# Attention scores on the two row halves of the TensorE array: eight heads per unit in place of four

## The chip, the cores and the metric

The kernel runs on one core of a Trainium2 chip. The metric is the device time of one execution in microseconds (us); lower is better. Engines are named as in the profile: PE is TensorE (PEld its weight loads), DVE is VectorE, ACT is ScalarE, POOL is GpSimd, SP issues DMAs.

## The reference

Thirty-two batches of 128 tokens of width 512 go through a layernorm, a cross-attention with 32 heads of width 16, a residual, a second layernorm and a mixture of eight experts with two chosen per token. The part that matters here is the attention of one batch: own keys and values, and a second set (the adapter's) from `ctx`, with its own softmax and a gate per head.

```python
scores = einsum('bhqd,bhkd->bhqk', q, k) * inv_sqrt_d + attention_mask
w = softmax(scores)
attn_output = einsum('bhqk,bhkd->bhqd', w, v)
a_scores = einsum('bhqd,bhkd->bhqk', q, a_k) * inv_sqrt_d
a_scores = tanh(gate) * softmax(a_scores)
attn_output = attn_output + einsum('bhqk,bhkd->bhqd', a_scores, a_v)
return attn_output.transpose(0, 2, 1, 3).reshape(bsz, q_len, hid) @ Wo
```

## The kernel before

Two phases: attention with the router, one batch of 128 tokens per step, then the experts, 71 slots of 128 tokens. The change touches the first. Its order is written out by hand: each engine has a function `step(b, c, d, n, m)` that is called for each batch b, and in it works on b, on the batch before (d), the one before that (c), the next (n) and the one after (m). Engines meet at semaphores (`wait_ge`, `then_inc`); an engine that waits holds everything behind it in its own order.

**Heads as pairs.** Queries and keys are split into two float16 parts, so a head takes 64 rows: two heads, a pair, fill the 128 partitions. `stack` (PE, L1084) transposes two pairs of queries, keys and adapter keys at a time (group g, four heads) into bank ma0 or ma1; `stack_out` (ACT, L553 and L555) copies them to qz and kk. In qz an even head has its rows 0 to 63 and zeros below, an odd head rows 64 to 127 and zeros above, so both use the same full-height key block.

**Maxima for n.** `adapter_scores` (L1108) and `own_scores` (L1117) make the scores of group g with queries on the partitions in md1 and md0; `maxima` (DVE, L754, L756, L759) adds the mask and takes the maximum over keys. PE's scores of group g wait for DVE's maxima of group g-1, since the banks are the same. `neg_max` splits minus the maxima into three bfloat16 parts, `max_turn` turns them, and mT holds them with heads on the rows.

**Transposed scores for b.** Units u = 0 to 15: g = u // 2 is the group of four heads, path = u % 2 is own or adapter. `scores_T` (L1143 to L1152) fills bank st[path]: two matmuls of 256 columns for the scores, on path 0 two of 512 for the mask (`mskp`, in two parts), and four of 128 that subtract the maximum through the selector `hsel`. `exps` (ACT, L561) takes the exponential of the bank to pr; `values` (L1166) multiplies by the values, four heads in four column strips of the array. A unit's bank is filled again two units later, after the exponential of u-2.

PE's step goes through u = 0 to 15: scores of u, then what lies at that place of batches n and d, then `values(u-1)`:

```python
for u in range(2 * GROUPS):
    scores_T(b, u)
    ...
    if n and u in STACK_AT:
        stack(n, STACK_AT.index(u))
    if n and u in SCORES_AT:
        adapter_scores(n, SCORES_AT.index(u))
    if u:
        values(b, u - 1)
    ...
```

Ahead of u = 0 is the query projection of n (`q`), at u = 2 the key projection `k`, at u = 3 the output projection of d, at u = 4 the adapter's keys `ak`, at u = 7 `h_turn`, at u = 8 `router`, and after u = 15 the values' projection `v`, `adapter_scores(7)`, `values(15)`, `own_scores(7)`, the adapter's values `avp` and `max_turn`. `v` waits for `stack_out` of group 6, the last user of ma0. `normal` (DVE) divides by the sums, eight heads at a time (o), after `values_back`. Lines are those of the kernel before.

Of the kernel before, what the change touches and what calls it, by code (L numbers as in the profile page):

```python
# [45 lines left out]
STACK_AT = (6, 7, 8, 9, 10, 11, 13, 15)  # L46
SCORES_AT = (8, 9, 10, 11, 12, 13, 14)
# [56 lines left out]
def attention_phase(nc, ctx, dram, keep):  # L104
# [25 lines left out]
    hsel = sb("hsel", [3 * NH, NH], BF16)  # L130
# [24 lines left out]
    mx = sb("mx", [P, 2, NH], F32)  # L155
    mr = sb("mr", [P, 2, NH], F32)
    mp = sb("mp", [P, 2, 3, NH], BF16)
    mT = sb("mT", [3 * NH, 2, P], BF16)
# [205 lines left out]
    def _(pool):  # L364
# [124 lines left out]
    def _(act):  # L489
# [56 lines left out]
        def stack_out(n, g):  # L546

            act.wait_ge(t_pe.sem, t_pe.at(n.shift(-1), 2 * g + 2))
            act.wait_ge(stk_t.sem, stk_t.at(n, g + 1))
            bank, pairs = half(ma[g % 2]), slice(2 * g, 2 * g + 2)  # L550
            for j in range(2):
                r = slice(64 * j, 64 * j + 64)
                act.activation(qz[r, pairs, j, :], bank[r, 0:2], ACT.Copy)  # L553
            keys = bank[:, 2:6].rearrange("p (k a) n -> p k a n", k=2)
            act.activation(kk[:, :, pairs, :], keys, ACT.Copy).then_inc(stk_o.sem, 1)  # L555

        def exps(n, u):
            path = u % 2
            act.wait_ge(t_pe.sem, t_pe.at(n, u + 1))
            act.wait_ge(av_pe.sem, av_pe.at(n, u - 1))  # L560
            act.activation(pr[:, path, :, :], st[path][:, :, :], ACT.Exp).then_inc(p_ex.sem, 1)  # L561
# [103 lines left out]
    def _(dve):  # L665
# [30 lines left out]
        pool_c_all = 19  # L696
# [53 lines left out]

        def maxima(n, g):
            dve.wait_ge(s_pa.sem, s_pa.at(n, g + 1))
            dve.wait_ge(s_own.sem, s_own.at(n, g))
            dve.tensor_reduce(mx[:, 1, 4 * g:4 * g + 4], sm[1][:, :, :], AX.X, ALU.max).then_inc(s_ad.sem, 1)  # L754
# [4 lines left out]
            dve.tensor_reduce(mx[:, 0, 4 * g:4 * g + 4], sm[0][:, :, :], AX.X, ALU.max).then_inc(s_own.sem, 1)  # L759

        def neg_max(n, b=None):
# [4 lines left out]
            p3 = [mp[:, :, k, :] for k in range(3)]  # L766
# [13 lines left out]
            dve.tensor_copy(mT[:, :, :], m_bank()[0:3 * NH]).then_inc(m_T.sem, 1)  # L780

        def normal(n, o):

            bank = av[o % 2][:, :, :].rearrange("p (a g) (j c) -> p a (g j) c", a=2, c=VC)
# [3 lines left out]
            dve.tensor_tensor(rc[:, 1, :], rc[:, 1, :], tg[:, 8 * o:8 * o + 8], ALU.mult).then_inc(n_rg.sem, 1)  # L788
# [4 lines left out]
            if o == 0:  # L793
                if whole(n):
# [3 lines left out]
            dve.tensor_tensor(heads(on)[:, 8 * o:8 * o + 8, :], part2[:, 0, :, :], part2[:, 1, :, :],  # L798
                              ALU.add).then_inc(n_o.sem, 1)
# [235 lines left out]
    def _(pe):  # L1035
# [88 lines left out]
        def max_turn(n):  # L1124
            pe.wait_ge(mp3.sem, mp3.at(n))
            for path in range(2):
                i = pe.transpose(m_bank()[0:3 * NH, path, :], mp[:, path, :, :].rearrange("p a h -> p (a h)"),
                                 ident_bf[:, :])
            i.then_inc(mp_t.sem, 1)

        def scores_T(n, u):

            g, path = u // 2, u % 2
            if u == 0:
# [15 lines left out]
            for j in range(4):  # L1150
                h = 4 * g + j
                i = pe.matmul(bank[:, j, :], hsel[:, h:h + 1].to_broadcast([3 * NH, P]), mT[:, path, :],  # L1152
                              start=False, stop=(j == 3), skip_group_check=True)
            i.then_inc(t_pe.sem, 1)

        def values(n, u):
            g, path = u // 2, u % 2
# [4 lines left out]
            if u % 4 == 0:  # L1162
                pe.wait_ge(n_o.sem, n_o.at(n, u // 4 - 1))
            for j in range(4):
                h = 4 * g + j
                i = pe.matmul(av[u // 4 % 2][VC * j:VC * j + VW, 2 * path + g % 2, :], vv[:, n.par, path, h, :],  # L1166
                              pr[:, path, j, :], start=True, stop=True)
# [464 lines left out]
```

## Time and profile before

| | us |
|---|---|
| median of 3 runs | 2137.03 |
| lowest, highest | 2134.46, 2138.43 |
| the profiled execution's own time | 2133.7 |
| its span, first to last instruction | 2131.9 |

Busy over the span: PE 89%, PEld 55%, DVE 68%, ACT 57%, POOL 30%. The attention phase ends some 1645 us into the span. A busy share counts a matmul from its start to its modelled end; matmuls overlap, so the starts tell more than the share.

### The profile page before, as it was taken

How to read it: one execution, taken by the hardware profiler on the slowest of the kernel's cores; microseconds unless marked ns; L12 is line 12 of the kernel's file. 1: busy time of each engine (PE TensorE's matmuls, PEld its weight loads, DVE VectorE, ACT ScalarE, POOL GpSimd, SP SyncE). 2: the span in 40 equal slices, each digit the busy share in tenths (PEclk: the TensorE clock that was granted, in tenths of full speed). 3: DMA queues.
4: the chain of work that ended last, by engine and by line, in shares of the span. 5: the costliest groups of instructions: out<-in, count | busy, mean ns of one | idle time of the engine just before them, and what ended most of it. 6: DMA issues, size and time to landing. Idle time of an engine off the chain costs nothing. (4 is left out here: it accounts for less than half of the span.)

```text
span 2131.9 us, 54083 instructions
## 1 busy us (share of the span) xinstructions
PE 1900.5 (89%) x18697; PEld 1172.2 (55%) x18698; DVE 1452.3 (68%) x3621; ACT 1219.3 (57%) x2228; POOL 647.5 (30%) x667
## 2 busy tenths in 40 slices
PE   4898899989998999999899999999983799999997
PEld 2555555555554555555555555555551466666664
DVE  5577788888887888888788888888874333333332
ACT  4565566666665666666566666666662434434342
POOL 3123233222322222232222222222321344444443
PEclk8999999999999999999999999999996899999999
DMA  3011111111111111111111111111012444444443
GB/s 124 24 34 34 34 34 34 40 41 55 35 34 35 34 34 34 34 34 39 30 40 52 45 34 34 34 34 34 29 33 72 106 81 86 82 83 85 81 87 59
DMA packets 64040, 106.14 MB, mean 50 GB/s; under 512 B 19089, under 2 KB 23185, under 8 KB 63313
## 3 DMA queue, kind: packets, MB, share of 16 engines
q0 software_dynamic: 18144, 37.31, 9.7%
q1 hardware_dynamic: 45680, 65.96, 9.6%
q8 instruction: 136, 2.23, 0.4%
q14 instruction: 80, 0.65, 0.1%
HBM read 67.51 MB, written 35.72 MB: 48 GB/s over the span
## 5 line engine op out<-in xcount | busy, mean ns | idle before, releaser
L561 ACT ACTIVATE pr<-st 128x512 f32<-128x512 f32 x512 | 299.9, 592 | 202.9 <-PE st L1152 193.0
L1499 PE MATMUL y<-w1s,hgT 128*128 x1704 | 279.8, 314 | 3.7 <-ACT hgT L1413 3.7
L410 POOL TENSOR_TENSOR t<-t 128x512 f32<-128x512 f32 x32 | 50.4, 1575 | 668.6 <-DVE t L734 668.6
L754 DVE TENSOR_REDUCE mx<-md 128x4 f32<-128x512 f32 x256 | 176.6, 690 | 86.6 <-PE md L1108 71.9
L1166 PE MATMUL av<-pr,vv 128*17 128x128 f32 x4096 | 212.4, 278 | 17.5 <-ACT pr L561 17.1
L1499 PEld LDWEIGHTS y<-w1s,hgT 128*128 128x128 f16 x1704 | 164.4, 98 | 95.4 <-issue 4.1
L553 ACT ACTIVATE qz<-ma 64x256 f16<-64x256 f16 x512 | 191.7, 374 | 19.2 <-PE ma L1084 16.2
L1152 PE MATMUL st<-mT,hsel 96*128 96x128 bf16 x2048 | 201.8, 221 | 0.0
L1143 PE MATMUL st<-qz,kk 128*128 128x256 f16 x1024 | 197.8, 275 | 1.4 <-DVE mT L780 1.4
L759 DVE TENSOR_REDUCE mx<-md 128x4 f32<-128x512 f32 x256 | 177.0, 691 | 8.7
L1147 PE MATMUL st<-identr,mskp 128*128 128x512 f32 x512 | 182.3, 437 | 0.0
L1152 PEld LDWEIGHTS st<-mT,hsel 96*128 96x128 bf16 x2048 | 137.5, 98 | 75.7 <-issue 69.8
L756 DVE TENSOR_TENSOR md<-md,msk 128x512 f32<-128x512 f32 x256 | 177.1, 692 | 0.0
L1413 ACT ACTIVATE hgT<-px 128x1024 f16<-128x1024 f16 x71 | 72.7, 1024 | 155.7 <-PE px L1489 155.7
L555 ACT ACTIVATE kk<-ma 128x512 f16<-128x512 f16 x256 | 152.9, 597 | 3.0
L1518 PE MATMUL y<-w2s,yT 128*128 (+1 forms) x639 | 150.3, 379 | 0.9 <-DVE yT L1477 0.9
L1117 PE MATMUL md<-kk,qz 128*128 128x128 f16 x1024 | 101.1, 221 | 51.3 <-DVE mx L759 50.9
L1476 DVE COPY yT<-py 128x256 f16<-128x256 f16 x142 | 40.4, 284 | 148.2 <-PE py L1508 148.2
L405 POOL TENSOR_TENSOR xcs<-nat,xcs 128x512 f16<-128x512 f32 x31 | 36.0, 1162 | 300.3 <-ACT xcs L493 300.3
L1166 PEld LDWEIGHTS av<-pr,vv 128*17 128x17 f32 x4096 | 68.2, 95 | 103.2 <-issue 54.1
L1117 PEld LDWEIGHTS md<-kk,qz 128*128 128x128 f16 x1024 | 60.3, 97 | 110.1 <-issue 110.1
L1392 POOL DMA_INDIRECT out<-yo,dst x71 | 113.2, 1594 | 16.9 <-issue 12.6
(210 smaller groups left out, 3999.6 us busy)
## 6 DMA issues: line engine op xcount, KB each, us to landing
wst<-in_w SPq DMA_DIRECT2D x32, 352.0 KB, 3.2
cin<-in_ctx SPq DMA_DIRECT2D x32, 256.0 KB, 3.8
xin<-in_x SPq DMA_DIRECT2D x32, 256.0 KB, 3.4
xres<-in_x SPq DMA_DIRECT2D x32, 256.0 KB, 3.6
out<-x SPq DMA_DIRECT2D x32, 256.0 KB, 2.1
h_pairs<-ohs SPq DMA_DIRECT2D x32, 256.0 KB, 2.1
msk<-in_mask SPq DMA_DIRECT2D x32, 64.0 KB, 3.4
lrow<-lists SPq DMA_DIRECT2D x71, 1.0 KB, 3.5
```

Source lines behind the costliest of these rows:

```text
L553: act.activation(qz[r, pairs, j, :], bank[r, 0:2], ACT.Copy)
L555: act.activation(kk[:, :, pairs, :], keys, ACT.Copy).then_inc(stk_o.sem, 1)
L561: act.activation(pr[:, path, :, :], st[path][:, :, :], ACT.Exp).then_inc(p_ex.sem, 1)
L754: dve.tensor_reduce(mx[:, 1, 4 * g:4 * g + 4], sm[1][:, :, :], AX.X, ALU.max).then_inc(s_ad.sem, 1)
L756: dve.tensor_tensor(sm[0][:, :, :], sm[0][:, :, :], msk[:, n.par, :].unsqueeze(1).to_broadcast([P, 4, P]), ALU.add).then_inc(s_mask.sem, 1)
L759: dve.tensor_reduce(mx[:, 0, 4 * g:4 * g + 4], sm[0][:, :, :], AX.X, ALU.max).then_inc(s_own.sem, 1)
L1117: i = pe.matmul(sm[0][:, j, :], qz[:, h // 2, h % 2, :], kst[:, h // 2, :], start=True, stop=True)
L1143: pe.matmul(bank[:, 2 * j:2 * j + 2, :], keys[:, p, :], qz[:, p, :, :], start=(j == 0), stop=False, skip_group_check=True)
L1147: pe.matmul(bank[:, :, :], mskp[:, n.par, part, :], identr[:, :].unsqueeze(1).to_broadcast([P, 4, P]), start=False, stop=False, skip_group ...
L1152: i = pe.matmul(bank[:, j, :], hsel[:, h:h + 1].to_broadcast([3 * NH, P]), mT[:, path, :], start=False, stop=(j == 3), skip_group_check=True)
L1166: i = pe.matmul(av[u // 4 % 2][VC * j:VC * j + VW, 2 * path + g % 2, :], vv[:, n.par, path, h, :], pr[:, path, j, :], start=True, stop=True)
L1499: i = pe.matmul(y1[s.par][j][:, 0:F], hgT[:, s.par, a, c, :], w, start=(n == 0), stop=(n == 11))
```

## The change

A unit of scores now has eight heads of one path. Even heads of four pairs go to bank st0 with array rows 0 to 63, odd heads to st1 with rows 64 to 127; each matmul has 64 rows and 128 columns, and the two halves alternate. The maxima are laid out likewise: even heads on rows 0 to 63 of mT, odd ones on 64 to 127, and `hsel` selects within a half. There are eight calls `scores_T(n, w)`, at the even places u = 2w; each raises `t_pe` twice. `exps` and `values` stay at sixteen, now with path = u // 2 % 2 and r = u % 2, the bank. `scores_T(w)` waits for both exponentials of w-1. The masks' matmuls of path 0 stand ahead of the scores. `stack_out(g)` waits for the scores of all eight heads that use its block, and stack 6 moves from u = 13 to u = 14, scores of group 6 from u = 14 to u = 15.

```diff
-STACK_AT = (6, 7, 8, 9, 10, 11, 13, 15)
-SCORES_AT = (8, 9, 10, 11, 12, 13, 14)
+STACK_AT = (6, 7, 8, 9, 10, 11, 14, 15)
+SCORES_AT = (8, 9, 10, 11, 12, 13, 15)
...
-        for part in range(3):
+        for k in range(6):
             const(pool.affine_select(out=hsel[:, :], in_=hsel[:, :], compare_op=ALU.not_equal, fill=1.0,
-                                     base=-NH * part, pattern=[[-1, NH]], channel_multiplier=1))
+                                     base=-(64 * (k // 3) + PAIRS * (k % 3)), pattern=[[-1, PAIRS]],
+                                     channel_multiplier=1))
+        const(pool.memset(mp[:, :, :], 0.0))
...
-            act.wait_ge(t_pe.sem, t_pe.at(n.shift(-1), 2 * g + 2))
+            act.wait_ge(t_pe.sem, t_pe.at(n.shift(-1), 4 * (g // 2) + 4))
...
-        pool_c_all = 19
+        pool_c_all = 23
...
+        def largest(path, g):
+
+            into = mx[:, 2 * path:2 * path + 2, 2 * g:2 * g + 2].rearrange("q r p -> q p r")
+            of = sm[path][:, :, :].rearrange("q (p r) k -> q p r k", r=2)
+            return dve.tensor_reduce(into, of, AX.X, ALU.max)
...
-        def scores_T(n, u):
-
-            g, path = u // 2, u % 2
-            if u == 0:
+        def scores_T(n, w):
+
+            o, path = w // 2, w % 2
+            if w == 0:
                 pe.wait_ge(m_T.sem, m_T.at(n))
                 pe.wait_ge(m_lo.sem, m_lo.at(n))
                 pe.wait_ge(m_hi.sem, m_hi.at(n))
-            if u >= 2:
-                pe.wait_ge(p_ex.sem, p_ex.at(n, u - 1))
-            bank, keys = st[path], (kst, akst)[path]
-            for j in range(2):
-                p = 2 * g + j
-                pe.matmul(bank[:, 2 * j:2 * j + 2, :], keys[:, p, :], qz[:, p, :, :], start=(j == 0), stop=False,
-                          skip_group_check=True)
+            else:
+                pe.wait_ge(p_ex.sem, p_ex.at(n, 2 * w))
             if path == 0:
-                for part in range(2):
-                    pe.matmul(bank[:, :, :], mskp[:, n.par, part, :],
-                              identr[:, :].unsqueeze(1).to_broadcast([P, 4, P]), start=False, stop=False,
-                              skip_group_check=True)
+                for r in range(2):
+                    for part in range(2):
+                        pe.matmul(st[r][:, :, :], mskp[:, n.par, part, :],
+                                  identr[:, :].unsqueeze(1).to_broadcast([P, 4, P]), start=(part == 0), stop=False,
+                                  skip_group_check=True)
             for j in range(4):
-                h = 4 * g + j
-                i = pe.matmul(bank[:, j, :], hsel[:, h:h + 1].to_broadcast([3 * NH, P]), mT[:, path, :],
-                              start=False, stop=(j == 3), skip_group_check=True)
-            i.then_inc(t_pe.sem, 1)
+                for r in range(2):
+                    rows, p = slice(64 * r, 64 * r + 64), 4 * o + j
+                    pe.matmul(st[r][:, j, :], (kst, akst)[path][rows, p, :], qz[rows, p, r, :],
+                              start=(path == 1 and j == 0), stop=False, skip_group_check=True)
+            for j in range(4):
+                for r in range(2):
+                    rows, p = slice(64 * r, 64 * r + 64), 4 * o + j
+                    i = pe.matmul(st[r][:, j, :], hsel[rows, p:p + 1].to_broadcast([64, P]), mT[rows, path, :],
+                                  start=False, stop=(j == 3), skip_group_check=True)
+                    if j == 3:
+                        i.then_inc(t_pe.sem, 1)
...
             for u in range(2 * GROUPS):
-                scores_T(b, u)
+                if u % 2 == 0:
+                    scores_T(b, u // 2)
```

The rest of the diff gives `mx`, `mr`, `mp`, `mT` and `hsel` the new layout and has `normal`, `values` and `exps` read heads in it; their counts and sizes stay, but for mT, which is copied with 128 rows in place of 96.

PE around u = 7 and 8, before (st is a bank of scores, L1174 is `values_back`, L1084 a stack, L1108 adapter scores for the maxima; `h_turn` and `router` stand here only where there is a batch d):

```order
L1143 MATMUL st<-qz,kk 128x256 x2
L1152 MATMUL st<-mT,hsel 128x128 x4
L1174 MATMUL av<-identr,avT 128x128 x4
L1084 MATMUL ma<-ident,qs 128x128 x2
L1084 MATMUL ma<-ident,ks 128x128 x2
L1084 MATMUL ma<-ident,aks 128x128 x2
L1166 MATMUL av<-pr,vv 17x128 x4
L1143 MATMUL st<-qz,kk 128x256 x2
L1147 MATMUL st<-identr,mskp 128x512 x2
L1152 MATMUL st<-mT,hsel 128x128 x4
L1084 MATMUL ma<-ident,qs 128x128 x2
L1084 MATMUL ma<-ident,ks 128x128 x2
```

and after (L1160 and L1165 are the scores and the maxima of a unit, L1154 the mask, L1096 a stack, L1120 adapter scores):

```order
L1187 MATMUL av<-identr,avT 128x128 x4
L1096 MATMUL ma<-ident,qs 128x128 x2
L1096 MATMUL ma<-ident,ks 128x128 x2
L1096 MATMUL ma<-ident,aks 128x128 x2
L1179 MATMUL av<-pr,vv 17x128 x4
L1154 MATMUL st<-identr,mskp 128x512 x4
L1160 MATMUL st<-qz,kk 128x128 x8
L1165 MATMUL st<-mT,hsel 128x128 x8
L1096 MATMUL ma<-ident,qs 128x128 x2
L1096 MATMUL ma<-ident,ks 128x128 x2
L1096 MATMUL ma<-ident,aks 128x128 x2
L1120 MATMUL md<-kk,qz 128x128 x4
```

Between stack 0 and the adapter scores of group 0 there were two units, of four heads each, one with and one without the mask; now there is one, with four mask matmuls and sixteen of 128 columns.

PE from the last scores of u = 14 to the values' projection, before (L1117 is own scores, L1045 on w_v the projection):

```order
L1152 MATMUL st<-mT,hsel 128x128 x4
L1174 MATMUL av<-identr,avT 128x128 x4
L1108 MATMUL md<-kk,qz 128x128 x4
L1166 MATMUL av<-pr,vv 17x128 x4
L1117 MATMUL md<-kk,qz 128x128 x4
L1143 MATMUL st<-qz,kk 128x256 x2
L1152 MATMUL st<-mT,hsel 128x128 x4
L1084 MATMUL ma<-ident,qs 128x128 x2
L1084 MATMUL ma<-ident,ks 128x128 x2
L1084 MATMUL ma<-ident,aks 128x128 x2
L1166 MATMUL av<-pr,vv 17x128 x4
L1045 MATMUL ma<-w_v,xT 128x512 x12
```

and after, from `values_back` at the same place (the unit of scores ahead of it is L1160 x8 and L1165 x8):

```order
L1187 MATMUL av<-identr,avT 128x128 x4
L1096 MATMUL ma<-ident,qs 128x128 x2
L1096 MATMUL ma<-ident,ks 128x128 x2
L1096 MATMUL ma<-ident,aks 128x128 x2
L1179 MATMUL av<-pr,vv 17x128 x4
L1096 MATMUL ma<-ident,qs 128x128 x2
L1096 MATMUL ma<-ident,ks 128x128 x2
L1096 MATMUL ma<-ident,aks 128x128 x2
L1120 MATMUL md<-kk,qz 128x128 x4
L1179 MATMUL av<-pr,vv 17x128 x4
L1129 MATMUL md<-kk,qz 128x128 x4
L1057 MATMUL ma<-w_v,xT 128x512 x12
```

The unit of u = 15 is gone, and stack 6 now stands here, two rows ahead of stack 7; the adapter scores of group 6, which read its copy, come right behind stack 7 and ahead of the projection.

## Rows read from the trace of the kernel before

**Rows 1.** The page, part 1: busy time of each engine, share of the span, instructions.

```profile
PE 1900.5 (89%) x18697; PEld 1172.2 (55%) x18698; DVE 1452.3 (68%) x3621; ACT 1219.3 (57%) x2228; POOL 647.5 (30%) x667
```

**Rows 2.** Waits of PE over the span: who for whom, total us, times, longest.

```profile
PE md L1117 <- DVE mx L759: 50.9, 130, 0.9
PE ma L1084 <- DVE aks L721: 37.6, 32, 2.6
```

**Rows 3.** Windows: stretch, its us, busy us (instructions) by engine, clock, DMA.

```profile
1389.33:1437.62 48.29, 44.50 (x483) 27.39 (x482) 40.47 (x94) 31.67 (x61) 12.94 (x11) 1.00 0.11 38
1415.08:1431.84 16.76, 15.12 (x209) 10.74 (x207) 15.90 (x29) 12.81 (x29) 3.31 (x4) 1.00 0.07 21
```

**Rows 4.** Timeline of PE, one step, first part: start us, us, instruction, [idle before].

```profile
1389.33 2.75 PE L1045 MATMUL ma<-w_q,xT 128*128 128x512 f16 x12
1391.92 0.38 PE L1143 MATMUL st<-qz,kk 128*128 128x256 f16 x2
...
1392.85 0.38 PE L1143 MATMUL st<-qz,kk 128*128 128x256 f16 x2
...
1393.86 0.41 PE L1166 MATMUL av<-pr,vv 128*17 128x128 f32 x8 [0.40 <-ACT pr L561]
...
1395.14 2.75 PE L1045 MATMUL ma<-w_k,xT 128*128 128x512 f16 x12
...
1403.94 2.75 PE L1045 MATMUL ma<-w_k,cT 128*128 128x512 f16 x12
```

**Rows 5.** Timeline of ACT in the same step: exponentials, adapter keys.

```profile
1393.13 1.09 ACT L561 ACTIVATE pr<-st 128x512 f32<-128x512 f32 x2 [1.80 <-PE st L1152]
...
1406.73 1.02 ACT L519 ACTIVATE aks<-ma 128x1024 f16<-128x1024 f32 x1 [1.70 <-PE ma L1045]
```

**Rows 6.** Timeline of PE in the same step, middle part.

```profile
1410.05 0.27 PE L1084 MATMUL ma<-ident,qs 128*128 128x128 f16 x2 [1.08 <-DVE aks L721]
...
1410.47 0.41 PE L1166 MATMUL av<-pr,vv 128*17 128x128 f32 x8
1410.82 0.39 PE L1143 MATMUL st<-qz,kk 128*128 128x256 f16 x2
...
1411.27 0.61 PE L1174 MATMUL av<-identr,avT 128*128 128x128 f32 x4
...
1413.86 0.45 PE L1045 MATMUL md<-rw,hT 128*128 128x8 f16 x12
1414.17 0.27 PE L1084 MATMUL ma<-ident,qs 128*128 128x128 f16 x2
...
1414.66 0.38 PE L1108 MATMUL md<-kk,qz 128*128 128x128 f16 x4
```

**Rows 7.** Timeline of ACT in the same step: first stack copied out, exponential.

```profile
1410.58 0.77 ACT L553 ACTIVATE qz<-ma 64x256 f16<-64x256 f16 x2 [0.35 <-PE ma L1084]
1411.36 0.60 ACT L555 ACTIVATE kk<-ma 128x512 f16<-128x512 f16 x1
1411.85 0.59 ACT L561 ACTIVATE pr<-st 128x512 f32<-128x512 f32 x1
```

**Rows 8.** Timeline of DVE in the same step: adapter keys, maxima of groups 0, 4.

```profile
1408.51 1.28 DVE L721 SCALAR_TENSOR_TENSOR aks<-ma,aks 128x512 f16<-128x512 f32 x2
...
1415.08 0.69 DVE L754 TENSOR_REDUCE mx<-md 128x4 f32<-128x512 f32 x1 [0.57 <-PE md L1108]
...
1424.62 0.69 DVE L754 TENSOR_REDUCE mx<-md 128x4 f32<-128x512 f32 x1
```

**Rows 9.** Timeline of PE in the same step, last part.

```profile
1422.53 0.38 PE L1117 MATMUL md<-kk,qz 128*128 128x128 f16 x4 [0.60 <-DVE mx L759]
...
1426.78 0.38 PE L1117 MATMUL md<-kk,qz 128*128 128x128 f16 x4 [0.40 <-DVE mx L759]
...
1430.49 2.76 PE L1045 MATMUL ma<-w_v,xT 128*128 128x512 f16 x12
```

**Rows 10.** Timeline of POOL at the program's start.

```profile
6.57 0.92 POOL L385 TENSOR_SCALAR_AFFINE_SELECT hsel<-hsel 96x32 bf16<-96x32 bf16 x3
```

More of the change, by code:

```diff
@@ L129, in attention_phase @@
     ones = sb("ones", [P, P], BF16)
-    hsel = sb("hsel", [3 * NH, NH], BF16)
+    hsel = sb("hsel", [P, PAIRS], BF16)
     rope = sb("rope", [P, 4, HD], F32)
@@ L154, in attention_phase @@
     vv = sb("vv", [P, 2, 2, NH, VW], F32)
[L155 to L158, printed above, removed]
+    mx = sb("mx", [P, 4, PAIRS], F32)
+    mr = sb("mr", [P, 4, PAIRS], F32)
+    mp = sb("mp", [P, 2, P], BF16)
+    mT = sb("mT", [P, 2, P], BF16)
     pr = sb("pr", [P, 2, 4, P], F32)
@@ L557, in exps @@
         def exps(n, u):
-            path = u % 2
+            r = u % 2
             act.wait_ge(t_pe.sem, t_pe.at(n, u + 1))
             act.wait_ge(av_pe.sem, av_pe.at(n, u - 1))
-            act.activation(pr[:, path, :, :], st[path][:, :, :], ACT.Exp).then_inc(p_ex.sem, 1)
+            act.activation(pr[:, r, :, :], st[r][:, :, :], ACT.Exp).then_inc(p_ex.sem, 1)
         def values_T(n, o):
@@ L753, in maxima @@
             dve.wait_ge(s_own.sem, s_own.at(n, g))
-            dve.tensor_reduce(mx[:, 1, 4 * g:4 * g + 4], sm[1][:, :, :], AX.X, ALU.max).then_inc(s_ad.sem, 1)
+            largest(1, g).then_inc(s_ad.sem, 1)
             dve.wait_ge(s_po.sem, s_po.at(n, g + 1))
@@ L758, in maxima @@
             dve.wait_ge(s_mask.sem, s_mask.at(n, g + 1))
-            dve.tensor_reduce(mx[:, 0, 4 * g:4 * g + 4], sm[0][:, :, :], AX.X, ALU.max).then_inc(s_own.sem, 1)
+            largest(0, g).then_inc(s_own.sem, 1)
         def neg_max(n, b=None):
@@ L765, in neg_max @@
             dve.wait_ge(mp_t.sem, mp_t.at(n.shift(-1)))
-            p3 = [mp[:, :, k, :] for k in range(3)]
+            rows = mp[:, :, :].rearrange("q a (r k p) -> q (a r) k p", r=2, k=4)
+            p3 = [rows[:, :, k, :] for k in range(3)]
             dve.tensor_scalar(p3[0], mx[:, :, :], -1.0, None, ALU.mult).then_inc(m_part.sem, 1)
@@ L779, in neg_max @@
             dve.wait_ge(mp_t.sem, mp_t.at(n))
-            dve.tensor_copy(mT[:, :, :], m_bank()[0:3 * NH]).then_inc(m_T.sem, 1)
+            dve.tensor_copy(mT[:, :, :], m_bank()).then_inc(m_T.sem, 1)
         def normal(n, o):
-            bank = av[o % 2][:, :, :].rearrange("p (a g) (j c) -> p a (g j) c", a=2, c=VC)
+            bank = av[o % 2][:, :, :].rearrange("p (a r) (j c) -> p a (r j) c", a=2, c=VC)
+            gate = tg[:, 8 * o:8 * o + 8].rearrange("p (j r) -> p r j", r=2)
+            tgo = rc[:, 1, :].rearrange("p (r j) -> p r j", r=2)
+            mine, theirs = (part2[:, a, :, :].rearrange("p (r j) d -> p r j d", r=2) for a in range(2))
             dve.wait_ge(v_back.sem, v_back.at(n, o + 1))
@@ L787, in normal @@
             dve.wait_ge(n_rc.sem, n_rc.at(n, o + 1))
[L788 removed]
+            dve.tensor_tensor(tgo, tgo, gate, ALU.mult).then_inc(n_rg.sem, 1)
             dve.wait_ge(n_rg.sem, n_rg.at(n, o + 1))
@@ L797, in normal @@
                 dve.wait_ge(o_lo.sem, o_lo.at(n.shift(-1)))
-            dve.tensor_tensor(heads(on)[:, 8 * o:8 * o + 8, :], part2[:, 0, :, :], part2[:, 1, :, :],
-                              ALU.add).then_inc(n_o.sem, 1)
+            dve.tensor_tensor(heads(on)[:, 8 * o:8 * o + 8, :].rearrange("p (j r) d -> p r j d", r=2),
+                              mine, theirs, ALU.add).then_inc(n_o.sem, 1)
         def out_low(n):
@@ L1162, in values @@
             if u % 4 == 0:
-                pe.wait_ge(n_o.sem, n_o.at(n, u // 4 - 1))
+                pe.wait_ge(n_o.sem, n_o.at(n, o - 1))
             for j in range(4):
-                h = 4 * g + j
-                i = pe.matmul(av[u // 4 % 2][VC * j:VC * j + VW, 2 * path + g % 2, :], vv[:, n.par, path, h, :],
-                              pr[:, path, j, :], start=True, stop=True)
+                i = pe.matmul(av[o % 2][VC * j:VC * j + VW, 2 * path + r, :], vv[:, n.par, path, 8 * o + 2 * j + r, :],
+                              pr[:, r, j, :], start=True, stop=True)
             i.then_inc(av_pe.sem, 1)
```

5 lines of the change are left out of this document (2 added, 3 removed).

## The prediction

> **What bounds the kernel now.** I read the page first. PE is busy for 89% of the span [rows 1], which looks like a kernel bound by TensorE, and the change takes work from TensorE. So the next view is who PE waits for. Two waits lead: own scores wait for DVE's maxima, 50.9 us in 130 waits, and the first stack of each step waits for DVE's adapter keys, 37.6 us in 32 [rows 2]. A PE that waits there is held by DVE, and time that it saves ahead of such a wait is lost in it.
>
> Then one step, from one query projection to the next: 48.29 us, PE busy 44.50, DVE 40.47, ACT 31.67, the granted clock at 1.00 [rows 3], its level of 2.4 GHz. There are 31 such steps (the last batch has no next one). Inside it DVE works without a break from the maxima of group 0 to those of group 6, 16.76 us with 15.90 busy and the rest in its own turnarounds [rows 3]. The timeline then gives a ring of four stretches: PE's queries and first units up to DVE's adapter keys; stack 0 up to the adapter scores of group 0, where PE and ACT take turns [rows 6, 7]; DVE's maxima up to own scores 5 [rows 8, 9]; and PE alone from there to the values' projection and on to the next step [rows 9]. Behind that projection nothing of PE's work changes. A step gets longer or shorter by what happens to these four ends.
>
> **Prices.** Twelve matmuls of 512 columns take 2.59 us, 0.216 each [rows 4]. A unit without the mask, 2 x 256 and 4 x 128 columns, takes 0.45 [rows 6], so 128 columns cost 0.055. The unit with the mask takes 0.93 [rows 4], which is 0.45 + 2 x 0.216 + 0.05. Six transposes of a stack should take 0.33, but the values begin 0.42 behind them [rows 6]: 0.09 for going over to column strips. The eight matmul instructions of values then take 0.35 up to the next scores, 0.26 without a second change of 0.09 [rows 6], where one after another they would take 0.44. So parts of the array do run beside each other, and changing the division costs 0.09 each way. The Trainium skill, TensorEngine Tiling (Array Packing), Key Properties, says that a change of tiling mode drains the engine; the trace agrees for column strips with its 0.09, and no row here shows row halves.
>
> No row shows two row halves at work, so I bound it: 0.055 for a pair if they overlap fully, 0.11 if not at all. The router's twelve matmuls of 8 columns, each with a full weight load, start 0.026 apart (0.31 / 12) [rows 6], so two loads and two matmuls can be issued in 0.052, just under 0.055. I take full overlap: 16 matmuls in 0.44. The nearest row short of it is the strips' pitch, 0.26 / 8 = 0.033, which gives 0.52. The Trainium skill, TensorE: Matmul & The Clock Gate, section Measured speedup vs the span model, has four row tiles at 3.07 times instead of 4; an estimate from that page is 0.44 / 0.77 = 0.57 for the sixteen, and with it the sum below would end 24 us higher.
>
> The new unit with the mask: 4 x 0.216 + 0.05 + 0.09 (mask on the full array, scores on halves) + 0.44 = 1.44, and 0.09 more where work on the full array follows. Without the mask: 0.44, 0.09 at each end towards the full array. Per eight heads that is 2.06 in place of 2 x 0.93 + 2 x 0.45 = 2.76, a saving of 0.70. But both exponentials must be done before the banks are filled again: from the unit's end 0.28 to the first exponential (1392.85 to 1393.13), 0.49 to the second, 0.73 from its start to PE (1393.13 to 1393.86) [rows 4, 5]: 1.50 in all.
>
> **The sum, end by end.**
> 1. *Adapter keys.* Unit 0 now ends at 1391.92 + 1.44 = 1393.36, unit 1 starts 1.50 later and `k` at 1394.86 + 0.44 + 0.09 = 1395.39, 0.25 late. DVE has other work then, which covers that. The unit at u = 3 goes, but PE waits there for the copy of `oT`, which shifted with `k`. At u = 4 the unit is 1.44 + 0.09 in place of 0.93: `ak` starts 0.85 late. ACT's adapter keys (1406.73, 1.02 long [rows 5]) end at 1408.60; DVE began its own part at 1408.51 [rows 8]. With 0.05 for the signal: **+0.15**.
> 2. *Stack 0 to adapter scores 0.* From stack 0: 0.53 to ACT's copy, 1.27 of copies to the exponential of u = 7, 0.73 to PE [rows 6, 7]. Now the unit at u = 8 waits for exactly that exponential, and PE, without unit 7, is there no later: 2.53, then 1.44 + 0.09 to the router: 4.06, against 3.81 (1410.05 to 1413.86). **+0.25**, and DVE's maxima begin that much later. What was saved, one unit, is what the eight heads with mask cost more.
> 3. *Maxima.* From own scores 3 to the maxima of group 4: 2.09 before (1422.53 [rows 9] to 1424.62 [rows 8]). Now 0.22 + 1.44 + 0.09, and 0.42 from adapter scores to DVE (1414.66 [rows 6] to 1415.08): 2.17. **+0.08**. The other saved units of this stretch fall into PE's waits for DVE and give nothing.
> 4. *Own scores 5 to the values' projection*, 3.71 before (1426.78 to 1430.49 [rows 9]). Now: own scores 0.22, change 0.09, unit 0.44, change 0.09, four transposes back 0.44 (four of 0.11), and stack 6 starts at 1.28. Its adapter scores need ACT's copy: 0.53 + 0.78 + 0.60, and 0.14 to PE [rows 5, 7], 2.05 in all, of which PE fills barely half with values 13 and stack 7. Then adapter scores, change, values 14 and own scores, 0.22 + 0.09 + 0.35 + 0.22 = 0.88, and `v` at 4.21. **+0.50**. Stack 6 used to stand a place earlier, where its copy cost nothing.
>
> Together +0.98 a step, 31 times: +30.4 us. At the start POOL makes three more selections (0.31 each [rows 10]) and one fill, and DVE, PE and ACT wait for all constants: +1.2. The DVE operations only write in another order, the same element counts: 0. The last step has no row here; I take it at 0, with 2 us either way. Sum 2133.7 + 31.6 = 2165.3 for the profiled execution, which lies 3.3 below the median of the runs shown; against that median **2168 us**, 1.5% slower. If changes of division and the 0.05 at the mask cost nothing, the ends are 0, +0.02, 0 and +0.32: 2148. If pairs start 0.066 apart, as the strips do, each new unit is 0.08 longer, and the ends are +0.39, +0.33, +0.16, +0.58: 2183.
>
> **Rivals.**
> - *The halves do not overlap*, the change doesn't do what it says: sixteen matmuls take 0.88. The ends become +1.46, +0.69, +0.52 and +0.94, 3.61 a step: 2250. Against it stands the overlap of the strips [rows 6]; for it, that the weights here have 128 columns, not 17, per load. The Trainium skill, TensorE: Matmul & The Clock Gate, section Back-to-back issue gap, gives about 81 ns for a matmul of 128 columns with its own load, so a pair would take 0.081 at best; the trace has 0.055 with a load each, so I don't take that price. 12%.
> - *The copy of stack 6 is not what ends last*, because ACT gets to it sooner or PE's work covers it. Then end 4 is PE's own work, 0.22 + 0.09 + 0.44 + 0.09 + 0.44 + 0.33 + 0.09 + 0.35 + 0.33 + 0.88 = 3.26, or -0.45, and the step is +0.03: 2140, no change. It decides where copy and signals take under 1.10 instead of 2.05; rows 7 speak against it. 8%.
> - *TensorE's work is the ring*, and it ends faster. Where the waits for DVE are slack that moves along with PE, the place is every unit and the price its whole saving, 4 x 0.70 = 2.8 a step: 2137 - 87 = 2050. For it: PE busy for 44.50 of 48.29. Against: DVE's unbroken stretch, and that own scores wait for maxima in four places. It decides only if DVE can begin group 0 earlier by what PE saves ahead of it, and end 2 says PE saves nothing there. 8%.
> - The rest, 6%: another wait of PE's for exponentials that I have as covered, at u = 6, 10, 12 or 14. Slower too, some 0.3 a step more.
>
> **Numbers.** 66% for my forecast, 2148 to 2183. The range also takes in the no-change case and, above, the page's estimate, 2139 to 2195; left out are the serial halves and the fast case. A measurement of this kernel can tell about 0.2% (4 us) from no change: faster 0.08, same 0.08, slower 0.84.
>
> **What would show it.** Starts of the scores' matmuls in pairs a few ns apart, eight pairs in 0.44. A unit with the mask of some 1.44. A new wait of some 0.9 us of PE, adapter scores of group 6 for ACT's `kk`, 31 times. PE's waits for exponentials at u = 2 and u = 8. PE's busy time lower although the span is longer. PE's wait for DVE's adapter keys shorter, since PE comes later, but not the keys earlier. Steps of 49.3 us. I am wrong if the step is under 48.3, if `v` starts less than 3.7 after own scores 5, or if the sixteen take 0.9.

## The result and the profile after

| | before | after |
|---|---|---|
| median, us | 2136.36 (4 runs) | 2181.07 (4 runs) |
| lowest, highest | 2134.46, 2138.43 | 2178.91, 2181.52 |
| the profiled execution: own time, span | 2133.7, 2131.9 | 2180.82, 2179.0 |
| regular step of the attention phase | 48.3 | 49.72 |

The ratio of after to before is 1.0216, 95% interval 1.0204 to 1.0228: 44.7 us slower. The prediction had 31 us more, 2168, and a range of 2139 to 2195.

The page of the changed kernel, part 1, answers to [rows 1]:

```profile
PE 1842.6 (85%) x19721; PEld 1107.1 (51%) x19722; DVE 1461.1 (67%) x3621; ACT 1221.0 (56%) x2228; POOL 645.6 (30%) x671
```

PE has 57.9 us less work and the kernel takes 47.1 us more of span. The waits of PE, who for whom, total us, times, longest, answer to [rows 2]:

```profile
PE md L1129 <- DVE mx L757: 61.7, 94, 0.9
PE md L1057 <- ACT oT L585: 36.7, 32, 2.1
PE md L1120 <- DVE mx L757: 34.6, 64, 3.6
PE st L1160 <- ACT pr L563: 32.7, 32, 1.0
...
PE md L1120 <- ACT kk L557: 23.5, 31, 2.6
...
PE ma L1096 <- DVE aks L723: 16.0, 32, 2.6
```

Two of these did not stand at the head of the list before: the scores' unit at u = 6 (L1160) waits for exponentials, and adapter scores 6 wait for ACT's copy of stack 6 (`kk`), 31 times. The wait for the adapter's keys (L1096) went from 37.6 to 16.0 us, and the keys came no earlier for it: PE came later. Where PE waits longest says where its saved work goes, not yet what makes the step longer. For that, one step is cut at the places that the prediction named. Window of one step, answering to [rows 3]:

```profile
1428.28:1478.00 49.72, 42.68 (x515) 25.37 (x513) 40.80 (x94) 31.73 (x61) 12.94 (x11) 1.00 0.11 37
```

PE is busy 1.82 us less in a step that is 1.43 longer. DVE's 40.80 and ACT's 31.73 have hardly moved, and the granted clock is 1.00, the level of 2.4 GHz, as before. The timeline of PE in this step, which answers to [rows 4, 6, 9]:

```profile
1428.28 2.75 PE L1057 MATMUL ma<-w_q,xT 128*128 128x512 f16 x12
...
1443.87 2.77 PE L1057 MATMUL ma<-w_k,cT 128*128 128x512 f16 x12
...
1448.24 0.40 PE L1160 MATMUL st<-qz,kk 64*128 64x128 f16 x8 [1.04 <-ACT pr L563]
...
1449.27 0.27 PE L1096 MATMUL ma<-ident,qs 128*128 128x128 f16 x2 [0.41 <-DVE aks L723]
...
1451.76 1.19 PE L1154 MATMUL st<-identr,mskp 128*128 128x512 f32 x4
1452.88 0.40 PE L1160 MATMUL st<-qz,kk 64*128 64x128 f16 x8
1453.11 0.39 PE L1165 MATMUL st<-mT,hsel 64*128 64x128 bf16 x8
1453.43 0.45 PE L1057 MATMUL md<-rw,hT 128*128 128x8 f16 x12
...
1454.23 0.38 PE L1120 MATMUL md<-kk,qz 128*128 128x128 f16 x4
...
1462.11 0.38 PE L1129 MATMUL md<-kk,qz 128*128 128x128 f16 x4 [0.60 <-DVE mx L757]
...
1466.65 0.38 PE L1129 MATMUL md<-kk,qz 128*128 128x128 f16 x4 [0.68 <-DVE mx L757]
...
1468.01 0.27 PE L1096 MATMUL ma<-ident,qs 128*128 128x128 f16 x2
...
1469.98 0.40 PE L1120 MATMUL md<-kk,qz 128*128 128x128 f16 x4 [0.68 <-ACT kk L557]
...
1470.89 2.75 PE L1057 MATMUL ma<-w_v,xT 128*128 128x512 f16 x12
```

Starts subtracted give the stretches between the ends; those of before come from [rows 4, 6, 9] in the same way:

| stretch | before | after | measured | forecast |
|---|---|---|---|---|
| 1, queries to stack 0 | 20.72 | 20.99 | +0.27 | +0.15 |
| 2, stack 0 to adapter scores 0 | 4.61 | 4.96 | +0.35 | +0.25 |
| 3, adapter scores 0 to own scores 5 | 12.12 | 12.42 | +0.30 | +0.08 |
| 4, own scores 5 to the values' projection | 3.71 | 4.24 | +0.53 | +0.50 |
| that projection to the next queries | 7.13 | 7.11 | -0.02 | 0 |

That is +1.43 in the regular step, which would be 44.3 us in 31 steps. The 31 stretches from one query projection to the next, summed in the view of windows, before and after:

```profile
sum 1513.79, PE 1370.84 PEld 840.33 DVE 1224.06 ACT 963.48 POOL 398.11; mean PE 44.22 PEld 27.11 DVE 39.49 ACT 31.08 POOL 12.84
sum 1555.70, PE 1315.27 PEld 778.65 DVE 1232.44 ACT 965.51 POOL 397.68; mean PE 42.43 PEld 25.12 DVE 39.76 ACT 31.15 POOL 12.83
```

They are 41.9 us apart, not 44.3: seven of the steps before take 48.5 to 48.6, and the first steps, in which not every batch is there yet, and the long ones differ by other amounts. The first query projection starts at 21.76 instead of 20.43, 1.33 later. From the last one to the end of the span it is 597.6 before and 601.5 after, 3.9 more; that part holds one more regular step, the last step and the experts. Together these are the 47.1 us between the two spans.

The same rows carry the prices. The eight matmuls of scores start at 1452.88 and the eight of maxima at 1453.11: 0.23 for four pairs, 0.058 a pair, where the trace of before has 0.055 for one matmul of 128 columns. So two row halves run fully beside each other. From there to the router 0.32, change of division included, so the sixteen with the change take 0.55. But the four mask matmuls take 1.12 (1451.76 to 1452.88), not 1.00. The unit is 1.67 long.

### The profile page after: what moved, and what is told of

Same layout as the page of the kernel before. It is cut to its first block and busy times, and to the rows that moved or that the text cites. A ratio compares the mean times of both kernels' runs of the same rounds, so it can differ in the third digit from the quotient of the medians.

```text
span 2179.0 us, 56138 instructions
## 1 busy us (share of the span) xinstructions
PE 1842.6 (85%) x19721; PEld 1107.1 (51%) x19722; DVE 1461.1 (67%) x3621; ACT 1221.0 (56%) x2228; POOL 645.6 (30%) x671
## 5 line engine op out<-in xcount | busy, mean ns | idle before, releaser
L1179 PE MATMUL av<-pr,vv 128*17 128x128 f32 x4096 | 204.9, 278 | 26.9 <-ACT pr L563 26.8
L1154 PE MATMUL st<-identr,mskp 128*128 128x512 f32 x512 | 156.4, 427 | 2.9 <-ACT pr L563 1.5
L1129 PE MATMUL md<-kk,qz 128*128 128x128 f16 x1024 | 101.7, 222 | 65.9 <-DVE mx L757 61.7
L1120 PE MATMUL md<-kk,qz 128*128 128x128 f16 x1024 | 100.7, 221 | 58.9 <-DVE mx L757 34.6
L1160 PE MATMUL st<-qz,kk 64*128 64x128 f16 x2048 | 101.9, 219 | 33.5 <-ACT pr L563 32.7
L1057 PE MATMUL md<-w_o,oT 128*128 128x512 f16 x384 | 90.8, 387 | 36.7 <-ACT oT L585 36.7
L1160 PEld LDWEIGHTS st<-qz,kk 64*128 64x128 f16 x2048 | 57.9, 94 | 105.4 <-ACT pr L563 51.9
```

The source lines that it names most:

```text
L1129: i = pe.matmul(sm[0][:, j, :], qz[:, h // 2, h % 2, :], kst[:, h // 2, :], start=True, stop=True)
L1154: pe.matmul(st[r][:, :, :], mskp[:, n.par, part, :], identr[:, :].unsqueeze(1).to_broadcast([P, 4, P]), start=(part == 0), stop=False, ski ...
L1160: pe.matmul(st[r][:, j, :], (kst, akst)[path][rows, p, :], qz[rows, p, r, :], start=(path == 1 and j == 0), stop=False, skip_group_check=True)
L1179: i = pe.matmul(av[o % 2][VC * j:VC * j + VW, 2 * path + r, :], vv[:, n.par, path, 8 * o + 2 * j + r, :], pr[:, r, j, :], start=True, stop ...
```

## The experiments

Each was timed beside the kernel before, whose median in the three groups of runs was 2135.36 (first four kernels), 2134.77 (next two) and 2135.25 (last two). Lines are those of each kernel.

### 1. Is it the alternation that makes the halves overlap?

```diff
-            for j in range(4):
-                for r in range(2):
+            for r in range(2):
+                for j in range(4):
```

in both loops of `scores_T`: four matmuls of one half, then four of the other.

> The changed kernel, but in each unit the four matmuls of rows 0 to 63 come first and then the four of rows 64 to 127, so pairs of halves can't run beside each other. If the overlap of pairs is what makes a unit short (0.054 us a pair in the changed kernel), sixteen matmuls take 0.8 to 0.86 in place of 0.43. Three units ahead of the adapter keys, and one in each of the other three ends of the step, are then 0.4 longer: the step goes from 49.72 to about 52.3, the time from 2181 to about 2260. If instead only the regrouping into eight heads (two exponentials to wait for) sets the time and PE's matmuls do not, the step stays within 0.3 of 49.7 and the time under 2192.

Measured: 2184.59 us in one run, step 49.81. Timeline of PE, the second unit of a step:

```profile
1435.71 0.41 PE L1160 MATMUL st<-qz,kk 64*128 64x128 f16 x8
1435.95 0.40 PE L1165 MATMUL st<-mT,hsel 64*128 64x128 bf16 x8
1436.28 1.04 PE L1057 MATMUL ma<-w_k,xT 128*128 128x512 f16 x4
```

Eight matmuls still take 0.24 and the unit is as long as with alternation, to 0.02. I had expected the halves to run one after another and was wrong. The experiment therefore took no overlap away and says nothing on what the overlap is worth; that fell to the next. What it does say stands in the last section.

### 2. What are the row halves worth in this order?

The same units, places, waits and exponentials, but each matmul over all 128 rows, as before the change. `qz` has zeros in the other half's rows already; the selector `hsel` gets them too and is twice as wide, and `unsel`, a small tile of the routing, shares the place of `wsel` to make room.

```diff
-                    rows, p = slice(64 * r, 64 * r + 64), 4 * o + j
-                    pe.matmul(st[r][:, j, :], (kst, akst)[path][rows, p, :], qz[rows, p, r, :],
+                    p = 4 * o + j
+                    pe.matmul(st[r][:, j, :], (kst, akst)[path][:, p, :], qz[:, p, r, :],
...
-                    i = pe.matmul(st[r][:, j, :], hsel[rows, p:p + 1].to_broadcast([64, P]), mT[rows, path, :],
+                    i = pe.matmul(st[r][:, j, :], hsel[:, r, p:p + 1].to_broadcast([P, P]), mT[:, path, :],
...
```

> The changed kernel's units of eight heads, order and waits, but every matmul over all 128 rows (the zeros in qz and in a wider selector do the selecting), as before the change: no halves, no change of the array's division between masks and scores and behind the unit. Sixteen matmuls of 0.055 are 0.88; a unit with masks 0.96 + 0.88 = 1.84 in place of the 1.66 measured (its change behind it included), one without 0.88 in place of 0.65. If that is all, the step is 49.72 + 0.6 (adapter keys) + 0.2 + 0.2 + 0.25 = 50.9 and the time about 2218, some 40 under the halves in turn, which pay 0.88 and the changes as well. If the changes of division are dearer than I read them, it comes close to 2181 or under it.

Measured: 2228.3 us in one run, step 51.29, stretches 21.86, 5.22, 12.67 and 4.43. Timeline of PE, the unit at u = 8 (one record of the mask's is missing):

```profile
1493.44 0.62 PE L1160 MATMUL st<-qz,kk 128*128 128x128 f16 x8
...
1494.34 0.45 PE L1057 MATMUL md<-rw,hT 128*128 128x8 f16 x12
```

Sixteen in 0.90, against 0.55 with the change of division. The halves save PE 2.22 us of busy time a step (44.90 here, 42.68 with them), and the step gets 1.57 of it, 47 us in all. So the change loses for its order, not for its halves: without the halves the same order would be 93 us behind the kernel before.

### 3. Is the copy of stack 6 what ends stretch 4?

The last unit of scores is issued at u = 13, ahead of own scores 5, so that all users of stack 6's keys are done earlier, and stack 6 is back at u = 13.

```diff
-STACK_AT = (6, 7, 8, 9, 10, 11, 14, 15)
+STACK_AT = (6, 7, 8, 9, 10, 11, 13, 15)
...
-                if u % 2 == 0:
+                if u % 2 == 0 and u != 14:
                     scores_T(b, u // 2)
...
+                if u == 13:
+                    scores_T(b, 7)
```

> The changed kernel, but the last unit of scores is issued at u = 13, behind values 12 and ahead of own scores 5, where PE waits 0.68 us for DVE, and stack 6 goes back to u = 13. My theory: the 0.53 us that the stretch from own scores 5 to the values' projection grew is the wait for ACT's copy of stack 6, and the last unit adds 0.65 that can be hidden. Then the stretch shrinks from 4.24 to about 2.6, the step to about 48.0, the time to about 2129, under the kernel before. Rival: DVE's maxima or the exponentials then end last there, and the stretch stays over 3.9; the step stays over 49.4 and the time over 2171.

Measured: median 2130.38 us (2126.13 to 2131.17, 6 runs), ratio to before 0.9969, interval 0.9956 to 0.9983; step 48.00. Its window, and PE's timeline at the end of the step:

```profile
1383.12:1431.12 48.00, 42.29 (x516) 25.26 (x513) 40.65 (x94) 31.63 (x61) 12.94 (x11) 1.00 0.11 38
```

```profile
1420.74 0.40 PE L1160 MATMUL st<-qz,kk 64*128 64x128 f16 x8
1420.97 0.39 PE L1165 MATMUL st<-mT,hsel 64*128 64x128 bf16 x8
1421.49 0.38 PE L1129 MATMUL md<-kk,qz 128*128 128x128 f16 x4
...
1422.94 0.40 PE L1120 MATMUL md<-kk,qz 128*128 128x128 f16 x4
...
1424.00 0.59 PE L1057 MATMUL ma<-w_v,xT 128*128 128x512 f16 x2
```

Own scores 5 to the values' projection is 2.51 (1421.49 to 1424.00), 1.73 shorter, and the wait for `kk` is gone. The other stretches are those of the changed kernel to 0.01: 20.99, 4.96, 12.42. One unit and one stack at other places, 51 us. The unit lies in time that PE had spent waiting for DVE ahead of own scores 5. Not all of the 1.73 is the copy. By the starts in the two timelines the wait for `kk` held PE for 0.85 (0.68 of it listed as idle), the unit with its changes took 0.65 and stack 6, which now stands a place earlier, some 0.4; a new gap ahead of values 14 gives 0.16 back. Two things moved at once, so the edit itself does not part them.

### 4. Can the mask's matmuls be hidden in the waits of u = 8 and u = 12?

At these two places the mask's four matmuls are issued alone, and the sixteen later, behind what DVE and ACT wait for.

```diff
+SPLIT_AT = (8, 12)
...
-                    scores_T(b, u // 2)
+                    (scores_mask if u in SPLIT_AT else scores_T)(b, u // 2)
...
+                if u in SPLIT_AT:
+                    if n and u == 8:
+                        own_scores(n, 0)
+                    scores_T(b, u // 2, True)
```

> The changed kernel, but at u = 8 and u = 12 a unit's four mask matmuls are issued by themselves where the unit was, and its sixteen others later: at u = 8 behind the router, stack 2 and the scores of group 0 for the maxima, at u = 12 behind adapter scores 4. My theory: stack 0 to adapter scores 0 grew by 0.35 and the maxima's stretch by 0.30 only because the whole unit stands in front of what DVE waits for. With the masks alone (0.96) in front, the router comes when ACT's copy for it is ready, 0.7 earlier, and the maxima's stretch is DVE's own again: step about 48.7, time about 2150. Rival: the exponentials of that unit, now 0.9 later, turn into waits of PE at u = 9 to 11 and give it back: step over 49.4.

Measured: median 2198.17 us (2188.13 to 2206.48, 4 runs), ratio 1.0306, interval 1.0277 to 1.0335. Timeline of PE after the first adapter scores of a step:

```profile
1512.25 0.38 PE L1121 MATMUL md<-kk,qz 128*128 128x128 f16 x4
...
1512.79 0.40 PE L1165 MATMUL st<-qz,kk 64*128 64x128 f16 x8
...
1515.85 0.40 PE L1165 MATMUL st<-qz,kk 64*128 64x128 f16 x8 [0.62 <-ACT pr L564]
```

Stretch 2 shrank as meant, from 4.96 to 4.35, and stretch 3 grew from 12.42 to 13.10. The exponentials of u = 8 and 9 follow the sixteen; these are later, so the unit at u = 10 now waits for them (in the list of waits 51.5 us in 62 times for L1165, where the changed kernel has 32.7 us in 32, all of them at u = 6), and with it everything behind it. The rival was right. The usual step is 49.77 and so no better; and some steps are 51.3, in which the granted clock was lower. Windows: such a step, a usual one, and ten microseconds out of the first:

```profile
419.82:471.15 51.33, 43.91 (x515) 26.39 (x513) 41.28 (x94) 31.64 (x61) 12.94 (x11) 0.97 0.11 35
370.05:419.82 49.77, 42.52 (x516) 25.35 (x513) 41.37 (x94) 31.64 (x61) 12.94 (x11) 1.00 0.12 36
450.00:460.00 10.00, 7.39 (x96) 4.95 (x93) 7.86 (x14) 5.95 (x13) 3.08 (x4) 0.83 0.01 0
```

The four runs' mean clocks were 0.973, 0.970, 0.962 and 0.968 with 2188, 2195, 2206 and 2201 us: the lower the clock, the longer the run. A mean of 0.83 over the ten microseconds means that part of them went by at 1.2 GHz; PE was busy for 7.39 of the 10.

### 5. Which of the other stretches can be given back?

On top of experiment 3: the mask apart at u = 12 alone, where nothing waits for its exponentials at once, and the adapter's keys ahead of the unit at u = 4, on PE and on ACT.

```diff
+                if u == 4 and n:
+                    ak(n)
                 if u % 2 == 0 and u != 14:
-                    scores_T(b, u // 2)
+                    (scores_mask if u in SPLIT_AT else scores_T)(b, u // 2)
...
-                if u == 4 and n:
-                    ak(n)
...
-                if u == 4 and n:
-                    ak_high(n)
...
                         k_high(n)
+                        ak_high(n)
```

> On top of the version with the last scores early (2130.4 us, step 48.00). Two edits. The adapter's key projection ak stands ahead of the scores' unit at u = 4 on TensorE, and ScalarE's copy of it ahead of exponential 4. At u = 12 the mask's four matmuls alone are issued first, adapter scores 4 next, the sixteen of scores and maxima behind. If stretch 1 (queries to stack 0) is set by the adapter's keys alone and the mask's matmuls at u = 12 lengthen stretch 3: stretch 1 loses the 0.27 that the change put there or more (ak stands 1.66 behind the unit now; what is gained ends at VectorE's own work before the keys), stretch 3 loses 0.1 to 0.2, the step is 47.6 and the time 2118 (2113 to 2123). Rival: the exponentials of units 4 and 5 come 1 us later behind the adapter's keys, the unit at u = 6 waits for them, and stack 0 is no earlier: step 48.0 or more, 2130 or above, with a wait for pr at L1160 or L1154 at u = 6.

Measured: median 2119.45 us (2117.12 to 2122.92, 6 runs), ratio 0.9925, interval 0.9913 to 0.9938; step 47.60, as forecast. Stretch 1 is 20.72, what it was before the change, and stretch 3 is 12.31; 4.96 and 2.49 are as in experiment 3. The timeline of PE:

```profile
1390.60 2.75 PE L1057 MATMUL ma<-w_k,cT 128*128 128x512 f16 x12
...
1396.23 0.40 PE L1164 MATMUL st<-qz,kk 64*128 64x128 f16 x8 [0.31 <-ACT pr L564]
...
1397.40 0.27 PE L1096 MATMUL ma<-ident,qs 128*128 128x128 f16 x2 [0.55 <-DVE aks L723]
```

The rival's wait for `pr` is there (0.31), and PE still waits 0.55 for the keys behind it, so it costs nothing. Stretch 1 shrank by just what the keys' lateness had put in: DVE's own work ahead of the keys ends it again.

### 6. Is it the order or the halves that now beats the kernel before?

Experiment 3 with every matmul over 128 rows, the edit of experiment 2.

> The version with the last scores early (2130.4 us, step 48.00), with every matmul of scores and maxima over all 128 rows: the same units, places and waits, but one after another and not in pairs. It parts what the row halves give from what the order gives. In the order of the change full height cost 1.6 us a step (51.31 against 49.72), 0.43 to 0.5 more per unit. If the halves are worth as much in this order, the step is 49.6 and the time 2181 (2172 to 2190): the row halves are then what puts this version ahead of the kernel before, and the order alone would lose. Rival: the early unit 7 took the halves' gain off the path at the end of the step (stretch 4), and only stretches 1 to 3 pay: step 49.0, 2160. If the order alone does it, 2130 to 2140.

Measured: median 2184.34 us (2182.4 to 2186.19, 4 runs), ratio 1.0233, interval 1.0218 to 1.0249; step 49.84, stretches 21.89, 5.23, 12.82, 2.78. PE at u = 8:

```profile
1452.84 1.21 PE L1154 MATMUL st<-identr,mskp 128*128 128x512 f32 x4
1453.89 0.62 PE L1160 MATMUL st<-qz,kk 128*128 128x128 f16 x8
...
1454.80 0.45 PE L1057 MATMUL md<-rw,hT 128*128 128x8 f16 x12
```

The halves are worth 54 us here, half of it in stretch 1. The order alone, with the regrouping and the mask at the head of the unit in it, loses 50 us to the kernel before; halves and order together win 5.0 (experiment 3). The rows also part the mask's price: 1.05 for four where no change of division follows them, 1.12 where one does.

### 7. Why do the mask's matmuls cost more than their columns?

The mask's high part in bfloat16; the low part, still of four bytes, takes the rest.

```diff
-    mskp = sb("mskp", [P, 2, 2, P], F32R)
+    mskh = sb("mskh", [P, 2, P], BF16)
+    mskp = sb("mskp", [P, 2, P], F32R)
...
-                        pe.matmul(st[r][:, :, :], mskp[:, n.par, part, :],
-                                  identr[:, :].unsqueeze(1).to_broadcast([P, 4, P]), start=(part == 0), stop=False,
+                        pe.matmul(st[r][:, :, :], (mskh, mskp)[part][:, n.par, :],
+                                  (ident_bf, identr)[part][:, :].unsqueeze(1).to_broadcast([P, 4, P]), start=(part == 0), stop=False,
```

> The changed kernel (2181.1 us, step 49.72) with the mask's high part in bfloat16 in place of the four-byte type; the low part, which takes what is left, stays as it is. It asks where the mask unit's extra time over the forecast comes from (1.66 from its start to the work behind it, forecast 1.53). Theory: the four-byte weight load of 0.19 starts only when the matmul ahead has started, so a mask matmul follows another after 0.23 to 0.24, not after the 0.216 of its 512 columns. With a two-byte load (0.09 to 0.10) before every other one, two of the four come after 0.216: the unit with the mask is 0.04 shorter, stretches 1 to 3 are 0.04 shorter each, the step 49.60, the time 2177 (2174 to 2180). Rival: the pitch does not come from the load (512 columns written to a bank, or the switch between banks): the unit, the step and the time stay within 0.01, 0.03 and 1 us.

Measured: median 2176.98 us (2173.57 to 2178.97, 4 runs), ratio 1.0199, interval 1.0182 to 1.0216; step 49.41, stretches 20.86, 4.86, 12.34, 4.23. The mask's block in PE's timeline, where each record now stands alone:

```profile
1446.20 0.39 PE L1155 MATMUL st<-ident_bf,mskh 128*128 128x512 bf16 x1
1446.24 0.58 PE L1155 MATMUL st<-identr,mskp 128*128 128x512 f32 x1
1446.66 0.39 PE L1155 MATMUL st<-ident_bf,mskh 128*128 128x512 bf16 x1
1446.70 0.58 PE L1155 MATMUL st<-identr,mskp 128*128 128x512 f32 x1
1447.21 0.40 PE L1161 MATMUL st<-qz,kk 64*128 64x128 f16 x8
```

and all the mask's weight loads over the span, with durations in ns, minimum, median, maximum:

```profile
L1155 PEld LDWEIGHTS st<-ident_bf,mskh x256: 95/96/151, 70.5 to 1642.8; 128*128 128x128 bf16 x128
...
L1155 PEld LDWEIGHTS st<-identr,mskp x256: 187/200/353, 70.8 to 1642.8; 128*128 128x128 f32 x128
```

The block takes 1.01 in place of 1.12, more than the 0.04 I expected for two replaced loads, and the stretches 1 to 3 are 0.13, 0.10 and 0.08 shorter. Where the gain falls shows beside the changed kernel, whose block starts at 1451.76; the timeline of its second pair of mask matmuls:

```profile
1452.32 0.62 PE L1154 MATMUL st<-identr,mskp 128*128 128x512 f32 x2
```

Its first pair takes 0.56 (1451.76 to 1452.32), its second 0.56 up to the scores (1452.32 to 1452.88), change of division included. Here the first takes 0.46 (1446.20 to 1446.66) and the second 0.55 (1446.66 to 1447.21). Both pairs lost a four-byte load, but almost all of the gain is in the first, whose first load stands behind column strips. So the load does set a price, but mostly once a block, where nothing long runs ahead of it. In the kernel before, the mask's first load stood behind 256 columns of scores; putting the mask behind the scores again was not tried. The medians differ by 4.1 us, less than 31 times 0.31; their ranges touch, so the step, read to 0.01, is the better measure of this edit. The Trainium skill, TensorE: Matmul & The Clock Gate, section Weight-path perf modes — Fast Weight Load (FWL) and DoubleRow, gives the faster weight load to 128 weights of any type but FP32; the trace agrees with 96 against 188 to 200 ns.

### 8. The best version

Experiment 5 with the edit of experiment 7.

> The same edit of the mask's high part on top of the version with the adapter's keys first (2119.5 us, step 47.61). If the mask unit is 0.04 shorter, only the unit at u = 8 and what lies ahead of the first stack count now, since at u = 12 the mask's matmuls stand apart from what follows and the keys were moved ahead of the unit at u = 4: step 47.5, time 2116 (2114 to 2120). Rival: nothing, 2119.5, if the load is not what sets the pitch.

Measured: median 2115.02 us (2112.21 to 2118.52, 4 runs), ratio 0.9901, interval 0.9885 to 0.9918; step 47.43, stretches 20.73, 4.85, 12.25, 2.48. This is 20 us faster than the kernel before. Stretch 1 did not move, as DVE sets it, and stretch 2 gave 0.11.

## Why the prediction came out as it did

The time was in the range, and the direction and the places were right. The forecast of +31 was 14 us short of +44.7.

- **What bounds the kernel.** The ring of stretches held: PE lost 1.82 us of busy time a step, and the step is the sum of the ends, not of the work. The rival in which TensorE's work is the ring, 2050, is out. Its price was too high as well: the prediction's saving of 0.70 per eight heads, 2.8 a step, had the mask too cheap and left out the change of division behind the unit with the mask.
- **Prices of halves.** Full overlap was right (0.058 a pair, 0.055 forecast), and the rival of serial halves is out. The estimate from the Trainium skill, TensorE: Matmul & The Clock Gate, section Measured speedup vs the span model, 0.57 for sixteen, would have put the sum at 2192, eleven above the measured time; the rows gave 0.23 for eight and speak for twice the rate. Change of division: the sixteen with it take 0.55, 0.53 forecast.
- **The mask: the step that failed.** "4 x 0.216 + 0.05": the 0.05 was booked once for a unit. It belongs to the matmuls. The rows of before had it: the unit with the mask takes 0.48 more than the one without, 0.24 for each of its two matmuls, where the projections' twelve give 0.216. I took the price from instructions with the same columns but a two-byte weight, and gave the remainder to the unit. Four then cost 0.96, not 0.91. The block measured 1.12, forecast 1.00, and the rest of the difference, some 0.07, is a term the sum did not have: the mask now stands at the head of the unit, behind column strips, and its first load is not covered. Experiment 7 finds it there: with a two-byte load first, the first pair takes 0.46 and not 0.56. The unit with its change came to 1.67 in place of 1.53. It enters stretches 1, 2 and 3 once each, and these were under by 0.12, 0.10 and 0.22. The shorter block of experiment 7 gives back 0.13, 0.10 and 0.08 there.
- **Stretch 3** was under by another 0.1. The sum had 2.17 from own scores 3 to the maxima of group 4 and nothing behind that. Measured, the maxima of group 4 begin 2.30 after own scores 3, and DVE, having stood idle for 0.32, comes to its next operation 0.67 later; in the unbroken run of before that took 0.60 (1424.62 [rows 8] to 1425.22). Timeline of DVE, one line of before and then the changed kernel:

```profile
1425.22 0.69 DVE L756 TENSOR_TENSOR md<-md,msk 128x512 f32<-128x512 f32 x1
...
1463.39 0.69 DVE L757 TENSOR_REDUCE mx<-md 128x4 f32<-128x512 f32 x1
1464.41 0.69 DVE L757 TENSOR_REDUCE mx<-md 128x4 f32<-128x512 f32 x1 [0.32 <-PE md L1120]
1465.08 0.70 DVE L764 TENSOR_TENSOR md<-md,msk 128x512 f32<-128x512 f32 x1
```

- **Stretch 4** was right by its own steps: stack 6 starts 1.36 after own scores 5 (1.28 forecast), the copy holds PE until 1.97 after it (2.05), and `v` follows 0.91 later (0.88). In experiment 3 the wait is gone, and the stretch is PE's own work: forecast at 3.26, it came to 2.51, since the unit with its two changes, 0.62 of the 3.26, and the six transposes of stack 6, 0.33, left the stretch too. Of the 0.20 by which it is over the remaining 2.31, 0.16 is the gap ahead of values 14.
- **The start** was +1.33 for +1.2. The 31 steps were +41.9, which is less than 31 times the regular step's +1.43, and what lies behind the last query projection was +3.9, with one regular step in it, where the sum took the last step at nothing and left the experts out; how much of it is the last step and how much the experts was not taken apart.
- **What would show it.** Most signs that were named are there: the pairs, the wait for `kk` 31 times (0.68 in this step, forecast 0.9), less busy time over a longer span, a shorter wait for the keys. The waits for exponentials named at u = 2 and u = 8 are not in the list as such: PE reaches the unit at u = 8 just as its exponential ends. The one that came, at u = 6, 32 times, the prediction had as covered. It costs nothing here, since stack 0 waits another 0.41 for the keys behind it. One size was off: the unit with the mask takes 1.58 without the change behind it (1.67 less 0.09), not 1.44, and the step is 49.7, not 49.3.

## What to carry to other kernels

A packing that halves an engine's time for an operation pays only where that engine sets the step; cut the step at its waits, and count what the coarser unit makes later (here a unit, a stack and the wait for the stack's copy, 1.7 us a step) before counting what it saves. When such a change loses, undo first its order and then its packing: here the packing was worth 47 to 54 us all along, and one unit and one stack issued earlier turned the loss into a gain. Take the price of a matmul from a row with the same weight type, not from one with the same columns, and with the same kind of work ahead of it.

## What the runs showed of the hardware beyond what was expected

- Matmuls on different row halves run beside each other even if four of one half stand ahead of all four of the other in the program: eight in 0.24 in experiment 1, like the 0.23 with alternation. The Trainium skill, TensorE: Matmul & The Clock Gate, section The mechanism, has matmuls start in strict program order. Experiment 1 speaks against that across row halves: in strict order its eight would have paired at most at the seam. That holds if the order of the program is the order in which TensorE got them; the trace has starts only. How far ahead TensorE takes them was not tried.
- A four-byte weight load of 0.19 to 0.20 costs most at the head of a block. In a row of matmuls of 512 columns it makes the pitch 0.24 in place of 0.216. At the head, behind column strips, a two-byte load in its place made the first pair 0.10 shorter (0.46 against 0.56), while the same exchange inside the block made the second pair 0.01 shorter (0.55 against 0.56).
- In experiment 4 the granted clock fell to a mean of 0.83 over a stretch of ten microseconds in which PE was busy for 7.39, inside a step of 51.33. In the kernel before three of the 31 steps are long and at a mean of 0.94 (55.32, 52.63 and 52.79 us), and the other kernels have such steps too. In experiment 4 four more, such as this one, are 1.5 us longer than the usual step, at 0.97, and that version differs from the changed kernel only in the order of its instructions. It is not alone in this: the profiled execution of experiment 7 has one such step, 51.06 at 0.97. Why the clock fell there was not settled.
